# A three-round graph kernel on one core: another block order in the third round, an earlier turn of each round's first block, the verdict inside the round, and one engine that waits for the output

## The reference

```python
h = jnp.maximum(_layernorm(x), 0.0)
agg_src  = segment_sum(h[src], dst); agg_edge = segment_sum(edge_attr, dst)
x = x + relu(concat([h, agg_src, agg_edge]) @ W.T + b)          # layer 0
h = jnp.maximum(_layernorm(x), 0.0)
h = relu(mean_agg(h) @ W1_l + b1 + h @ W1_r)                    # layer 1, first half
x = x + relu(mean_agg(h) @ W2_l + b2 + h @ W2_r)                # layer 1, second half
```

## Time and profile before

| what | value |
|---|---|
| median of three runs | 1465.26 us (1460.28 to 1466.94) |
| profiled execution: own time / span | 1467.45 us / 1465.7 us |
| granted TensorE clock, mean | 0.976 of 2.4 GHz |
| TensorE busy over the span | 1364.9 us (93%) |
| GpSimd busy | 656.8 us (45%) |
| VectorE / ScalarE busy | 817.0 us (56%) / 485.4 us (33%) |
| gathers of listed blocks | 555 DMAs, 976 ns mean on GpSimd |

### The profile page before, as it was taken

The page is one execution under the profiler, slowest core; times in us unless marked ns, Lnnn a source line. Parts: engine busy times, 40 slices in busy tenths (PEclk is TensorE's granted clock), DMA queues, the critical chain, the costliest instruction groups (busy, mean ns, idle before and its releaser), DMA issues.

```text
span 1465.7 us, 34654 instructions
## 1 busy us (share of the span) xinstructions
PE 1364.9 (93%) x12165; PEld 1232.6 (84%) x12166; DVE 817.0 (56%) x1839; ACT 485.4 (33%) x1388; POOL 656.8 (45%) x770
## 2 busy tenths in 40 slices
PE   3686999999999999998999999999999999899986
PEld 3565999999999999997888888888888888788875
DVE  7678998888888888882545455422222222112111
ACT  2450123456678888881332323211111110000000
POOL 4410000011112122126777777077777726777773
PEclk9698999999999999999999999999999999999998
DMA  6107778888889898885564647456566746657662
GB/s 179 27 4 214 202 219 230 238 249 241 260 261 274 265 278 256 265 263 196 168 223 159 232 139 227 151 185 214 185 214 194 203 155 205 222 178 227 206 171 74
DMA packets 284747, 295.13 MB, mean 201 GB/s; under 512 B 19445, under 2 KB 250048, under 8 KB 284656
## 3 DMA queue, kind: packets, MB, share of 16 engines
q1 hardware_dynamic: 235541, 213.75, 46.7%
q0 software_dynamic: 26016, 69.24, 16.7%
q10 hardware_dynamic: 23099, 10.89, 2.6%
HBM read 245.70 MB, written 48.11 MB: 200 GB/s over the span
## 4 chain that ended last, share of the span: by engine, by line
PE 74%; POOL 11%; issue 6%; DVE 5%; ACT 2%; DMA 1%; ACTq 0%; DVEq 0%; POOLq 0%
PE edge_banks L1036 30%; PE edge_banks L1001 19%; PE banks L975 11%; POOL shared L813 11%; PE edge_banks L1067 3%; PE edge_banks L997 3%; PE banks L1054 3%; ACT shared L1210 1%; PE banks L891 1%; PE edge_banks L1043 1%; ACT banks L1205 1%; PE banks L1048 1%; DMA shared<-g_rows,list_src 1%; DVE edge_t L1370 1%; DVE g_even L1434 0%
## 5 line engine op out<-in xcount | busy, mean ns | idle before, releaser
L813 POOL DMA_INDIRECT shared<-g_rows,list_src x555 | 541.8, 976 | 235.1 <-issue 167.8
L1036 PE MATMUL edge_banks<-g_even,shared 128*128 128x257 f16 (+1 forms) x3822 | 445.4, 273 | 5.4 <-DMA shared<-counts 4.5
L1036 PEld LDWEIGHTS edge_banks<-g_even,shared 128*128 128x128 fp8e3 x3822 | 372.7, 98 | 64.3 <-issue 4.7
L1001 PE MATMUL edge_banks<-shared 128*128 128x128 f32 x2744 | 339.9, 276 | 0.0
L1001 PEld LDWEIGHTS edge_banks<-shared 128*128 128x128 f32 x2744 | 323.6, 193 | 0.0
L792 POOL DMA_DIRECT2D counts<-shared x156 | 76.4, 490 | 473.5 <-ACT shared L1210 458.4
L1588 DVE SCALAR_TENSOR_TENSOR shared<-edge_banks,shared,own 128x128 f32<-128x128 f32 x98 | 34.4, 351 | 374.3 <-PE edge_banks L1036 335.8
L1036 PE MATMUL edge_banks<-shared 128*128 128x256 f16 x1911 | 225.8, 272 | 0.9 <-DVE own L1570 0.9
L1514 DVE TENSOR_TENSOR shared<-iota,shared 128x3528 f16<-128x3528 f16 x98 | 195.5, 1995 | 48.3 <-PE banks L975 48.2
L1210 ACT ACTIVATE shared<-banks 128x392 uint16<-128x392 f32 x312 | 152.3, 488 | 186.9 <-PE banks L975 177.0
L1036 PEld LDWEIGHTS edge_banks<-shared 128*128 128x128 fp8e3 x1911 | 185.3, 97 | 31.3 <-DVE own L1570 1.2
(11 more groups left out here) (277 smaller groups left out, 987.2 us busy)
## 6 DMA issues: line engine op xcount, KB each, us to landing
shared<-in_edge_attr SPq DMA_DIRECT2D x195, 512.0 KB, 4.5
shared<-counts SPq DMA_DIRECT2D x117, 784.0 KB
counts<-shared POOLq DMA_DIRECT2D x156, 196.0 KB, 3.9
shared<-g_rows,list_src POOLq DMA_INDIRECT x555
shared<-hot_rows SPq DMA_DIRECT2D x20, 304.0 KB, 3.0
g_rows<-g_even SPq DMA_DIRECT2D x1, 3136.0 KB, 15.6
g_rows<-shared ACTq DMA_DIRECT2D x49, 64.0 KB
g_rows<-g_even ACTq DMA_DIRECT2D x49, 64.0 KB
```

Source lines behind the costliest of these rows:

```text
L813: pool.indirect_dma_start(ring_g[use % RING][:, t, 0:2 * D], None, g_rows[r], bass.IndirectOffsetOnAxis(ap=list_src[:, at:at + 1], axis=0) ...
L1001: mm = pe.matmul(edge_wide[bank][:, :, at], ring[:, bank * GROUP_TILES + j, :], hot_dst[u][:, k, (j - 1) * SPREAD:j * SPREAD].unsqueeze(1) ...
L1036: mm = pe.matmul(acc[s][:, 0:wide], stream8[slot][:, order[h], :], G[r % 2][:, order[h], 0:wide], start=h == 0, stop=h == BLOCKS - 1, skip ...
```

## The change

It does four things.

1. `LIST_AT` becomes one tuple for each round. Rounds one and two keep theirs. Round three has (6, 11, 16, 21, 25, 30, 35, 40, 45, 48): its last block is a listed one. Functions that find a block's place, number or store take the round as an argument. In round three the stores are one more (28).
2. In the first block of rounds two and three, `turn` comes after 34 matmuls in place of 39, and after 12 in place of 24; `dense` comes 6 matmuls behind the turn in place of after the 46th.
3. TensorE's sum of the check totals is issued behind place 37 of round three, and VectorE's 11 instructions stand ahead of place 41, with the verdict's semaphore right behind them.
4. ScalarE no longer waits for the output stores. SP still does.

```diff
-LIST_AT = (6, 11, 15, 20, 25, 29, 34, 38, 43, 47)
+LIST_AT = ((6, 11, 15, 20, 25, 29, 34, 38, 43, 47),) * 2 + ((6, 11, 16, 21, 25, 30, 35, 40, 45, 48),)
...
+        NEW_TURN, NEW_DENSE = (34, 12), 6
+        SUMS_AT, VERDICT_AT = 37, 41
...
-                        turn_at = LATE_SPLIT if r == (1 if i == 0 else 0) else SPLIT
+                        turn_at = NEW_TURN[r - 1] if new else LATE_SPLIT if r == 0 else SPLIT
+                        dense_at = turn_at + NEW_DENSE if new else last
...
-                        sums(turn_at, last)
+                        sums(turn_at, dense_at)
                         if 1 in turns:
                             dense(1)
+                        if dense_at < last:
+                            sums(dense_at, last)
                         for h in range(last, BLOCKS):
...
-                pe.wait_ge(S["sums_ready"], 1)
-                pe.matmul(banks[0:1, 2, 0:8], ones[:, 0:1], totals, start=True, stop=True).then_inc(S["sums_up"], 1)
+                        if r == 2 and i == SUMS_AT:
+                            pe.wait_ge(S["sums_ready"], 1)
+                            pe.matmul(banks[0:1, 2, 0:8], ones[:, 0:1], totals, start=True, stop=True).then_inc(S["sums_up"], 1)
...
-                act.wait_ge(R["out_stored"], 16 * OUT_STORES)
...
+                        if r == 2 and i == VERDICT_AT:
+                            judge()
+                            dve.sem_inc(S["verdict"], 1)
                         one(i)
```

More of the change, by code:

```diff
@@ L590, in message_passing, with is_listed, place_of @@
         SCHUNKS = -(-SBLK // 4)
[L592 to L596, removed]
+        DENSE_AT = [[i for i in range(BLOCKS) if i not in at] for at in LIST_AT]
+        for at in LIST_AT:
+            assert len(at) == LISTED and min(at) >= 6 and min(b - a for a, b in zip(at, at[1:])) >= 3
+        assert LIST_AT[0][-1] == LIST_AT[1][-1] == BLOCKS - 2 and SUMS_AT not in LIST_AT[2] and VERDICT_AT not in LIST_AT[2]
+        def is_listed(r, i):
+            return i in LIST_AT[r]
         def list_of(k):
             return k // 2 + (0 if k % 2 else LISTED // 2)
-        def place_of(i):
-            return DENSE + list_of(LIST_AT.index(i)) if is_listed(i) else DENSE_AT.index(i)
+        def place_of(r, i):
+            return DENSE + list_of(LIST_AT[r].index(i)) if is_listed(r, i) else DENSE_AT[r].index(i)
         def to_turn(i, r):
@@ L609, in to_turn, with before, after, sends @@
                 return (1,) if r > 0 else ()
[L610 to L618, removed]
+            return () if is_listed(r, i) else (2, 1) if is_listed(r, i - 1) else (1,)
+        def before(r, i, back):
+            return place_of(r, i - back) if i >= back else place_of(r - 1, i - back + BLOCKS)
+        def after(r, i):
+            return place_of(r, i + 1) if i + 1 < BLOCKS else place_of(r + 1, 0)
+        def sends():
+            held = []
+            for i in range(BLOCKS):
+                held.append(place_of(2, i))
+                if is_listed(2, i) or len(held) == 3 or i == BLOCKS - 1 or is_listed(2, i + 1):
+                    yield i, held[0], len(held)
+                    held = []
+        OUT_STORES = len(list(sends()))
         def number(r, i):
@@ L695, in one @@
                         n = number(r, i)
-                        if i > 0 and r == 0 and is_listed(i - 1):
-                            k = LIST_AT.index(i - 1)
+                        if i > 0 and r == 0 and is_listed(r, i - 1):
+                            k = LIST_AT[r].index(i - 1)
                             sp.wait_ge(R["list_hot"], k + 1)
                             sp.dma_start(hot_rows[k], list_hot_u8.rearrange("p t d -> p (t d)")).then_inc(S["hot_stored"], 16)
-                        if is_listed(i):
+                        if is_listed(r, i):
                             if r > 0:
-                                k = LIST_AT.index(i)
-                                last = number(r, LIST_AT[k - 1]) if k > 0 else number(r - 1, LIST_AT[-1])
+                                k = LIST_AT[r].index(i)
+                                last = list_number(list_use(r, k) - 1)
                                 sp.wait_ge(R["summed"], done_at(max(last, n - 4)))
@@ L1027, in one @@
                         turns = to_turn(i, r) if r < 2 or i == 0 else ()
-                        order = [place_of(k) for k in range(BLOCKS)] if new else range(BLOCKS)
+                        order = [place_of(r - 1, k) for k in range(BLOCKS)] if new else range(BLOCKS)
                         last = BLOCKS - 3 if new else NEAR_END
@@ L1241, in high @@
                             o = (s + back) % 2
-                            at = block_at(before(i, back))
+                            at = block_at(before(r, i, back))
                             act.wait_ge(R["g_up"], n + 1 - back)
@@ L1246, in one @@
                         if r == 0:
-                            copy_edge(after(i), n + 1, 1 - s)
-                        if is_listed(i):
+                            copy_edge(after(r, i), n + 1, 1 - s)
+                        if is_listed(r, i):
                             turned(1)
@@ L1258, in store @@
                         def store(back):
-                            b = before(i, back)
+                            b = before(r, i, back)
                             act.wait_ge(R["g_done"], n + 3 - back)
@@ L1285, in send @@
                     act.dma_start(rows.rearrange("(b p) f -> p b f", p=P), blocks).then_inc(R["out_stored"], 16)
-                stores, held = 0, []
-                for i in range(BLOCKS):
-                    if is_listed(i) and place_of(i) == BLOCKS - 1:
+                for i, b, n in sends():
+                    if b == BLOCKS - 1:
                         act.wait_ge(R["fin"], i + 1)
                         act.dma_start(out[(BLOCKS - 1) * P:N], x_sb[0:TAIL, BLOCKS - 1, :]).then_inc(R["out_stored"], 16)
[L1291 to L1298, removed]
-                act.wait_ge(R["out_stored"], 16 * OUT_STORES)
+                    else:
+                        send(i + 1, b, n)
             with act.If(go > 0):
@@ L1634, in rounds @@
                         dve.wait_ge(S["inv_ready"], 1)
[L1635 to L1646, removed]
             with dve.If(go > 0):
```

48 lines of the change are left out of this document (31 added, 17 removed).

## The result

The changed kernel takes **1452.8 us** (median of four runs, 1452.01 to 1453.23) against 1465.9 us before (the three runs known and a fourth of 1466.57); the ratio is 0.9912, with a 95% interval of 0.9892 to 0.9931. It is faster, by 13.1 us; forecast were 13.4 us and 1451.9 us. The profiled execution took 1453.23 us, its span 1451.5 us, 14.2 less than before.

A forecast was written before the change was run, and what follows sets the result against it. Round three was taken as bound by TensorE's work and GpSimd's gather pace, paid one behind the other. Rounds gain 7.6 us and the end 5.8, so 1465.26 - 13.4 = 1451.9 us, range 1446 to 1460.

The forecast's parts named there:

- The bound: Round three: GpSimd's gather pace of 1.25 us alone sets the end in the new order; TensorE has 5 us of slack.
- Early turn, round two: First block of round two: dense comes after 40 matmuls instead of 46, moving all behind it by 0.65 us.
- Early turn, round three: First block of round three: dense moves up 2.9 us, the stores and first gather follow, the latter to 1209.05.
- The order: Round three's new list places: waits at 15 and 38 go, 5 us at 48; final x 7.6 us earlier, at 1447.2.
- L: Time from the start of a list's last gather to TensorE's first matmul, put between 2.8 and 4.9 us.
- The verdict: VectorE's 11 instructions at place 41 of round three: hidden beside TensorE's dense block, costing up to 1.5 us if not.
- The end: Behind final x: no engine waits for the verdict, GpSimd's 7.74 us DRAIN is hidden; 5.8 us less.
- The lock: VectorE's checks beside round three's first gathers might delay GpSimd: taken as 0, 1.5 us left for the range.
- A: Rival at the end: GpSimd's DRAIN can't begin before other work is over; only 7.5 us less, 1457.8 us; chance 0.10.
- B: Rival in round three: waits eat the order's gain, some 5 to 7 us lost, about 1459 us; chance 0.08.
- C: Rival in round three: clock stays low behind the wait at place 25, kernel slower, 1471 us or beyond; chance 0.03.
- D: Rival for the whole kernel: no change, as runs differ by 6.7 us and the gain is overrated; chance 0.03.

The follow-up runs named there:

- g1_hold: `b1_after` with SP's load of counts for place 3 of round three held until all 49 row stores have landed: median 1457.1 us, ratio 0.9932.
- g2_hold_late_turn: `g1_hold` with the late turn (after 39 and 24 matmuls, dense after the 46th): median 1462.4 us, ratio 0.9970.
- r1_old_order: `b1_after` with only round three's order of listed blocks put back to the old one: median 1463.4 us, ratio 0.9967.
- b1_after: Changed kernel plus the study's shared edit, waits in the building of the tables against max(value, 1): median 1457.7 us, ratio 0.9932 to the kernel before.
- b0_before: Kernel before the change plus the study's shared edit, waits in the building of the tables against max(value, 1): median 1471.6 us, ratio 1.0026.
- r2_late_turn: `b1_after` with only the turn put back (after 39 and 24 matmuls, dense after the 46th): median 1462.1 us, ratio 0.9952.
- r3_verdict_end: `b1_after` with TensorE's sum and VectorE's 11 verdict instructions put back behind the rounds: median 1465.0 us, ratio 0.9982.

## Why the prediction was right, point by point

- **The bound.** That GpSimd's pace, not TensorE, sets round three's end with the new order: shown by `g1_hold` against `g2_hold_late_turn`, where a first gather 3.0 us earlier ends the span 3.0 us earlier, and by TensorE's 7.15 us wait in the changed kernel, which costs nothing as long as the gathers are under way. That the old order pays for its dense block behind the last list is shown by `r1_old_order`. No run changed the pace of the gathers itself.
- **Early turn, round two:** 0.65 us reckoned, 0.9 measured; the like pairs of the study gave 0.7 (`g1_hold`, `g2_hold_late_turn`) and 1.2 us (`b1_after` against `b0_before` and against `r2_late_turn`).
- **Early turn, round three:** dense was issued 3.1 us earlier (1203.77 against 1206.86), of which 0.1 is the start of the round; the first gather came 3.4 us earlier than in the trace of before, 3.55 reckoned, and 0.36 of that is the last store, which took 3.42 us in place of 3.78. The size was right, and `g1_hold` and `g2_hold_late_turn` show it clean. The prediction missed that the store's landing jumps between 1.5 and 3.8 us; it took the 3.78 of one trace as given, and luck had the store land late in the changed kernel's trace as well.
- **The order:** final x was at 1446.9, reckoned 1447.2. TensorE's way there was off, which the gathers' pace covers: the wait at place 25 was 0.54 us and not 2 to 4 (TensorE came 1.1 us later, and L was 2.7 us with no load just ahead), and at place 30, where none was forecast, it waited 0.61 us. So TensorE was at place 48 at 1434.4 and not at 1436.8, and waited 7.15 us, not 5. L there was 1441.54 - 1438.88 = 2.7 us, taken as 2.8. The list took 4.2 us, taken as 3.8, and VectorE's first op followed by 0.1 us, taken as 0.3: two small errors of opposite sign.
- **The verdict:** hidden, as predicted: VectorE's 11 instructions ran from 1400.99 to 1402.56, it then stood idle for 2.68 us, and TensorE had no wait behind place 40 until the last list.
- **The end:** of the 13.4 us reckoned 5.8 were to come from here, and 7.6 from the rounds; 6.3 and 7.9 were measured. GpSimd's DRAIN ended at 1447.4, reckoned 1447.9. ScalarE and VectorE needed 3.5 and 4.3 us behind their last work, in place of 4.55 and 4.9. TensorE's way was wrong by 5 us without effect. The prediction let the loading of the verdict and the branch follow the end of the list, but TensorE's sequencer is ahead of its matmuls: it branched at 1442.5, 1 us behind the first matmul of the last list, and its DRAIN stood at 1446.0, not 1451.3.
- **The lock:** none. VectorE's checks ran from 1208.90 to 1211.9 beside the first gathers, as the timeline of the changed kernel has it:

```profile
1208.90 0.32 DVE L1561 CAST shared<-row_sum 128x312 int32<-128x312 f32 x1
1209.17 0.94 POOL L830 DMA_INDIRECT shared<-g_rows,list_src  x1 [24.96 <-DMA g_rows<-g_even]
...
1210.24 0.47 DVE L1566 TENSOR_REDUCE few<-shared 128x1 f32<-128x312 int32 x1
1210.41 0.94 POOL L830 DMA_INDIRECT shared<-g_rows,list_src  x1 [0.30 <-issue]
```

  No gather got longer. The lock that the Trainium skill describes ("SBUF — State Buffer", section on the two separate sides of SBUF) fits the gather of 2.94 us in round one only, beside the 2.68 us instruction; these instructions of 0.3 to 0.5 us don't show it, and no run tells whether their length or their form is the reason.
- **The rivals.** A is out: the DRAIN ended at 1447.4, 3.8 us before VectorE reached its own, and `r3_verdict_end` shows what it costs when it is reached late. B is out: L at place 48 was 2.7 us, no gather got longer, and the early turn gave its full amount; only the list was near its upper bound, with 4.2 us. C did not arise: the wait at place 25 was 0.54 us. Where waits of 4.8 and 5.3 us did stand in the middle of the round, in `r1_old_order`, the four dense blocks behind the list took 22.1 and 22.0 us in place of 21.8; the granted clock was 0.50 through the list at place 15, 0.65 over the next microsecond and 1.00 in the one after it. D is out: the slowest run of the changed kernel, 1453.23 us, is faster than the fastest of the one before, 1460.28.

The early part of the sum rests on one execution of each kernel, in which the last store happened to land late both times. In `b0_before` it landed early, in `b1_after` late, and the same change gave 11.1 us behind M. What share of the runs of the kernel before has the quick landing isn't known, so that the total came out within 1 us is in part luck.

## What to carry to other kernels

Look at what each engine does behind its last piece of work: a closing step of fixed length on one engine (here 7.7 us on GpSimd) costs nothing if that engine isn't made to wait for a late flag, and the flag can often be made early. Where one engine feeds another at a fixed pace, count when the n-th piece can be there and put the consumer's last piece at the end; waits earlier in the order then cost nothing as long as the consumer still reaches that last piece before it is there. And look for large loads beside the one small transfer that everybody waits for: here such a load made a store of 1.5 us last 3.4 to 3.8.

## What was not expected of the hardware

- GpSimd's closing DRAIN takes 7.74 us when the engine has been idle for 10 us or more (three profiles), and ends 7.6 to 7.7 us behind the last gather when it is reached early (the other eleven). It is no wait for the other engines; what it does in that time isn't shown.
- A 64 KB store lands in 1.5 us with no large load of counts ahead of it and in 3.4 to 3.8 us with one. For a gather it matters how far ahead the load was issued: L was 2.7 us where the load was 3.2 us ahead of it (place 25 of the changed kernel), 3.3 us at 2.7 us (place 30), and 4.4 to 5.0 us at 1.1 us or less (place 11 there, and places 15 and 38 of the old order).
- A sequencer that is ahead of its engine's work hides its own branch: in the kernel before TensorE's stood alone, from 1457.4 on, and took 4.4 us; in the kernel after it began at 1442.5, took 3.4 us, and lay beside the last list's matmuls (1441.54 to 1445.75). The rows of its line, of before and after:

```profile
L1109 PEldq COMPARE_BRANCH  x1: 4415/4415/4415, 1457.4 to 1457.4; - x1
```

```profile
L1130 PEldq COMPARE_BRANCH  x1: 3389/3389/3389, 1442.5 to 1442.5; - x1
```
